# Two attention blocks and a routed expert layer on one core: projections in halves over two steps, a first expert round one step later, group sums copied inside two chains

## The reference, cut to what matters

```python
def reference(x, ...):
    # 1: causal attention over 2048 rows, rotary positions, 16 heads of 8
    x = layernorm(x + attn(x))                 # Q, K, V, softmax(QK/sqrt(8)) V, @ Wo
    # 2: attention over all rows (no mask), then one of 8 experts for each row
    f = x + msa(layernorm(x, ln1), w_qkv, w_proj)
    h = layernorm(f, ln2)
    e = argmax(h @ gate_w + gate_b)            # 8 experts
    f = f + gelu(h @ w1[e]) @ w2[e]            # 128 -> 512 -> 128
    return layernorm(x + f)
```

## Time and profile before

| | |
|---|---|
| median of three runs | 914.34 us (913.54 to 917.52) |
| the profiled execution | 915.0 us, its span 913.3 us (1.7 us lie around it) |
| PE, ACT, DVE, POOL busy | 819.6, 777.6, 328.7, 223.1 us |
| mean granted clock of TensorE | 0.953 of 2.4 GHz |

### The profile page before, as it was taken

One profiled execution on the slowest core, in us unless ns is written; L12 is line 12 of the kernel. 1 busy time (PEld: TensorE's weight loads), 2 busy tenths in 40 slices (PEclk: granted clock), 3 DMA queues, 4 the chain that ended last, 5 costly groups with the idle time before them and its releaser, 6 DMA issues.

```text
span 913.3 us, 24231 instructions
## 1 busy us (share of the span) xinstructions
PE 819.6 (90%) x9924; PEld 372.1 (41%) x9936; DVE 328.7 (36%) x948; ACT 777.6 (85%) x913; POOL 223.1 (24%) x359
## 2 busy tenths in 40 slices
PE   6689899999999999999999999999999999996271
PEld 3344344444444444444343444443444434443231
DVE  3711644410431005330042333264332463334753
ACT  1568789899999999999999999998999999994460
POOL 4732131111100110000003333323234132343333
PEclk9789999999999999999999999999999999998586
DMA  8976120202020250720201000201000010001101
GB/s 264 271 222 197 48 78 17 94 2 48 1 94 1 70 118 2 249 76 2 47 2 32 1 2 4 76 10 33 2 3 19 14 42 2 2 3 31 38 5 41
DMA packets 34357, 51.60 MB, mean 57 GB/s; under 512 B 4032, under 2 KB 14656, under 8 KB 34240
## 3 DMA queue, kind: packets, MB, share of 16 engines
q1 hardware_dynamic: 32704, 46.30, 17.7%
q0 software_dynamic: 1536, 3.67, 1.3%
HBM read 29.12 MB, written 20.84 MB: 55 GB/s over the span
## 4 chain that ended last, share of the span: by engine, by line
PE 58%; issue 21%; DVE 8%; ACT 5%; DMA 3%; POOL 3%; POOLq 2%; ACTq 0%; SPq 0%; DVEq 0%
PE ps L479 54%; ACT probs L864 3%; PE ps L484 2%; POOLq L999 2%; PE ps L738 1%; DMA early_late<-z_sorted 1%; POOL parts L1006 1%; DMA z_sorted<-z_rows,slot_numbers 1%; DVE ln_newton L1068 1%; POOL z_sorted L977 1%; DVE squares_blockdiag L1353 0%; DVE ln_newton L1067 0%; DMA early_late<-in_sin 0%; DVE ln_newton L1066 0%; DVE squares_blockdiag L1352 0%
## 5 line engine op out<-in xcount | busy, mean ns | idle before, releaser
L864 ACT ACTIVATE probs<-ps 128x1024 f32<-128x1024 f32 (+3 forms) x832 | 732.6, 1014 | 52.7 <-PE ps L479 51.0
L479 PE MATMUL ps<-probs,values 128*9 128x256 f32 (+1 forms) x6528 | 429.3, 376 | 4.3 <-POOL probs L972 1.8
L479 PE MATMUL ps<-query_rows,key_rows 32*128 32x512 f32 (+3 forms) x1664 | 289.8, 486 | 16.2 <-ACT probs L864 12.0
L479 PEld LDWEIGHTS ps<-probs,values 128*9 128x9 f32 x6528 | 143.6, 90 | 184.4 <-issue 95.2
L479 PEld LDWEIGHTS ps<-query_rows,key_rows 32*128 32x128 f32 x1664 | 121.6, 183 | 195.2 <-issue 95.3
L972 POOL TENSOR_SCALAR_AFFINE_SELECT probs<-probs 128x256 f32<-128x256 f32 x128 | 53.1, 421 | 238.9 <-ACT probs L864 236.0
L1013 POOL COPY parts<-early_late 128x512 f32 x63 | 42.7, 716 | 147.5 <-PE ps L479 147.4
L977 POOL DMA_INDIRECT z_sorted<-z_rows,slot_numbers x16 | 15.8, 990 | 213.9 <-DVE slot_numbers L1341 204.4
L1209 DVE COPY q_rotated<-ps 128x512 f32<-128x512 f32 x30 | 20.7, 690 | 129.6 <-PE ps L479 129.6
L1006 POOL COPY parts<-parts 128x512 f32 x72 | 45.4, 671 | 29.6 <-PE ps L479 27.8
L1221 DVE RECIPROCAL recip<-ps 128x16 f32<-128x16 f32 x32 | 8.2, 256 | 82.1 <-PE ps L484 82.1
(11 more groups left out here) (171 smaller groups left out, 573.6 us busy)
## 6 DMA issues: line engine op xcount, KB each, us to landing
k_scratch<-parts SPq DMA_DIRECT2D x16, 512.0 KB, 3.8
q_scratch<-parts SPq DMA_DIRECT2D x16, 512.0 KB, 5.1
query_rows<-q_scratch SPq DMA_DIRECT2D x32, 256.0 KB, 5.3
key_rows<-k_scratch SPq DMA_DIRECT2D x20, 256.0 KB, 4.9
key_rows<-k_scratch SPq DMA_DIRECT2D x16, 192.0 KB, 4.5
parts<-in_w SPq DMA_DIRECT2D x1, 2048.0 KB, 8.3
early_late<-in_w SPq DMA_DIRECT2D x8, 256.0 KB, 7.1
early_late<-z_sorted SPq DMA_DIRECT2D x4, 384.0 KB, 3.2
```

The source lines that it names most:

```text
L479: return nc.tensor.matmul(out, l, r, start=start, stop=stop, skip_group_check=True)
L864: nc.scalar.activation(Pr[:, t % KEPT, 2 * p:2 * p + 2, lo:BLK], score_banks(t, p)[:, :, lo:BLK], ACT.Exp, bias=-SHIFT[r["a"]], scale=SCAL ...
```

## The change

- `post_project`, `m_gate` and the three `project2` functions take a half each time: two of four small matmuls, or 256 of 512 columns. The halves stand in two neighbouring steps. For keys, queries and values the second half has the step of `PREP_AT` and the first the step before; `post_project` is at steps 6 and 7 (it was at 6), `m_gate` at 11 and 12 (it was at 11). `m_turn` stays at 10 and `m_ranks` at 13.
- `UP_AT`, `TURN_AT`, `DOWN_AT` of the first round, the second round's `UP_AT` and `DOWN_AT` of the first, and `SORTED_AT`: one step later. Some places of `PREP_AT` too.
- On DVE the group's copy is written at new places: in attention 1 behind `bound_diag` and ahead of the wait for the bound's matmul; in attention 2 after the first of three Newton turns of the row norm, and again after the keys were rounded. A gelu of the expert rounds is written ahead of what is due in the step before `turn`.

```diff
-UP_AT = (25, 31, 38, 44, 50, 57)
+UP_AT = (26, 32, 38, 44, 50, 57)
-SORTED_AT = (22, 23)
+SORTED_AT = (23, 24)
...
+POST_TURN_AT, POST_AT, GATE_AT = 5, 7, 12
...
-            def project2_keys(b):
+            def project2_keys(b, n):
                 s = A[2]
-                turn_taken()
-                pe.wait_ge(hTs, b + 1)
-                mm(ps7, wqkv[:, D:2 * D], hT[:, :]).then_inc(s["k_proj"], 1)
+                c = slice(n * BLK // 2, (n + 1) * BLK // 2)
+                if n == 0:
+                    turn_taken()
+                    pe.wait_ge(hTs, b + 1)
+                last = mm(ps7[:, c], wqkv[:, D:2 * D], hT[:, c])
+                if n == 1:
+                    last.then_inc(s["k_proj"], 1)
...
-                todo = {5: [lambda: post_turn(n - 1)], 6: [lambda: post_project(n - 1)]}
+                todo = {POST_TURN_AT: [lambda: post_turn(n - 1)]}
+                for m in range(2):
+                    todo[POST_AT - 1 + m] = [lambda m=m: post_project(n - 1, (m,))]
...
-                    todo.update({10: [lambda: m_turn(b)], 11: [lambda: m_gate(b)], 13: [lambda: m_ranks(b)]})
+                    todo.update({10: [lambda: m_turn(b)], 13: [lambda: m_ranks(b)]})
+                    for m in range(2):
+                        todo[GATE_AT - 1 + m] = [lambda m=m: m_gate(b, (m,))]
...
-                rsqrt(y, v, h, t, 3)
+                rsqrt(y, v, h, t, 1)
+                between()
+                newton(y, h, t, 2)
...
                 ts(kdg[:, :], ident[0:H, 0:H], u, 1.03, ALU.mult, ALU.mult).then_inc(diag_set, 1)
+                between()
                 dve.wait_ge(bound_mm, a)
...
-                link(layernorm(xb, xb))
+                link(layernorm(xb, xb, lambda: due(10)))
...
                 link(copy(rounded(k3, b), ka[:, :]))
+                due(at[1] + 1)
...
-                        due(at - 1)
+                        due(at - 2)
                         gelu(b, r)
...
-                    bound(1)
+                    bound(1, lambda: due(BOUND1_AT))
```

More of the change, by code:

```diff
@@ L506, in turn_taken, with project2_queries, project2_values @@
                     pe.wait_ge(normed, turns[0])
[L508 removed]
+            def project2_keys(b, n):
                 s = A[2]
[L510 to L520 removed]
+                c = slice(n * BLK // 2, (n + 1) * BLK // 2)
[5 more added lines that the diff above has]
+                    last.then_inc(s["k_proj"], 1)
+            def project2_queries(b, n):
+                s = A[2]
+                c = slice(n * BLK // 2, (n + 1) * BLK // 2)
+                if n == 0:
+                    turn_taken()
+                    pe.wait_ge(s["k_taken"], b + 1)
+                last = mm(ps7[:, c], wqkv[:, 0:D], hT[:, c])
+                if n == 1:
+                    last.then_inc(s["q_proj"], 1)
+            def project2_values(b, n):
                 s = A[2]
[L522 to L524 removed]
+                if n == 0:
+                    turn_taken()
+                    pe.wait_ge(s["q_taken"], b + 1)
+                for i in (2 * n, 2 * n + 1):
                     last = mm(ps[:, 7, i * D:(i + 1) * D], hT[:, i * P:(i + 1) * P], wqkv[:, 2 * D:3 * D])
[L526 removed]
+                if n == 1:
+                    last.then_inc(s["v_proj"], 1)
             def key_norms(a, b):
@@ L670, in post_turn, with post_project @@
                 turned(ps7, lambda i: att[:, i, :]).then_inc(post_t, 1)
-            def post_project(n):
-                pe.wait_ge(post_e, n + 1)
-                for i in range(TB):
+            def post_project(n, halves=(0, 1)):
+                if 0 in halves:
+                    pe.wait_ge(post_e, n + 1)
+                for i in (i for m in halves for i in (2 * m, 2 * m + 1)):
                     last = mm(ps[:, 7, i * D:(i + 1) * D], attT[:, i * P:(i + 1) * P], (wo if n < NB else wproj)[:, :])
-                last.then_inc(post_p, 1)
+                if 1 in halves:
+                    last.then_inc(post_p, 1)
             def z_turn(b):
@@ L687, in m_turn, with m_gate @@
                 turned(ps7, lambda i: zb[:, i, :]).then_inc(m_zT, 1)
-            def m_gate(b):
-                pe.wait_ge(m_h, b + 1)
-                for i in range(TB):
+            def m_gate(b, halves=(0, 1)):
+                if 0 in halves:
+                    pe.wait_ge(m_h, b + 1)
+                for i in (i for m in halves for i in (2 * m, 2 * m + 1)):
                     last = mm(ps[:, 7, i * E:(i + 1) * E], hT[:, i * P:(i + 1) * P], gw[:, :])
-                last.then_inc(m_g, 1)
+                if 1 in halves:
+                    last.then_inc(m_g, 1)
             def m_ranks(b):
@@ L811, in side_of @@
                 b, at = n - 1, PREP_AT[n - 1]
-                ops = (z_turn, project2_keys, project2_queries, project2_values, lambda b: key_norms(2, b), lambda b: query_norms(2, b))
-                for p, f in zip(at, ops):
-                    todo[p] = [lambda f=f: f(b)]
+                for p, f in zip(at[1:4], (project2_keys, project2_queries, project2_values)):
+                    for m in range(2):
+                        todo[p - 1 + m] = [lambda f=f, m=m: f(b, m)]
+                todo.update({at[0]: [lambda: z_turn(b)], at[4]: [lambda: key_norms(2, b)], at[5]: [lambda: query_norms(2, b)]})
                 for i, p in enumerate(at[6]):
@@ L1064, in rsqrt, with newton @@
                 link(ts(h, v, -0.5, None, ALU.mult))
+                newton(y, h, t, turns)
+            def newton(y, h, t, turns):
                 for _ in range(turns):
@@ L1074, in layernorm, with normalize @@
                 link(ins)
-                return normalize(dst, src)
-            def normalize(dst, src):
+                return normalize(dst, src, between)
+            def normalize(dst, src, between=lambda: None):
                 for i in range(TB):
@@ L1130, in take_query_norms, with bound @@
                     link(tt(qmx[:, 0:1], qmx[:, 0:1], qmx[:, 1:2], ALU.max))
-            def bound(a):
+            def bound(a, between=lambda: None):
                 u, y, h, t = (bw[:, m:m + 1] for m in range(4))
@@ L1429, in attention @@
                         dve.sem_inc(mask_free, 1)
-                    due(10)
                     rows_to_h(n - 1, due)
```

8 lines of the change are left out of this document (4 added, 4 removed), and 4 rows, old and new, of the table PREP_AT.

## The result

The changed kernel takes 918.57 us in the median of five executions (918.28 to 926.73) against 914.34 (910.10 to 917.52) in five before, 4.2 us more. The ratio of all executions is 1.0076, with a 95% interval of 1.0044 to 1.0107, so the loss is clear of the noise.

A forecast was written before the change was run, and what follows sets the result against it. ACT was taken to set the pace, 1.83 us a step. Terms -3.1 - 3.1 + 0.6 - 0.7 - 1.15 + 0.8 + 3.6 = -3.05 took 915.0 to 911.95, 911.3 on the median's scale; 8-in-10 range 906.0 to 917.0.

The forecast's parts named there:

- the later round: Attentions 6 to 8, ahead of the second round's turn: the earlier gelu gives 0.1 us each, -0.3 in the sum.
- waits at `m_turn` and at the ranks: Attentions 6 to 8: PE waits 0.8 us at step 10 and 1.7 before the ranks, the latter taken as +1.8 each.
- low stretches behind the ranks: Attentions 6 to 8: a stretch of 0.50 clock follows the ranks' wait, 1.2 us each, +3.6 (bounds 0 and 5).
- Halves: the step that failed most: Splitting PE work over two otherwise plain steps gains about 0.4 us; output projection 2.4 in attentions 3 to 8, projections 1.55.
- I take no wait: Attentions 4 and 5: the first copy is due after the z rows are turned, or with room; attention 4 sums to -0.7.
- Steps 6 to 13 cancel: Attentions 6 to 8, up to step 13: output projection -0.4, wait at `m_turn` +0.8, gate -0.4 us, together 0.
- the three low stretches after the tanh stay: After the gelu's tanh PE idles 1.02 us, then gets 0.50 clock (values 1.90 instead of 1.05 us); this remains three times.
- Attention 2 (-3.1): Attention 2: norm wait about halved (-0.7), copy wait of 1.16 gone, queries -0.5, later halves and norms -0.7; bounds -1.2 and -4.3.
- the clock holds: Rival, chance 0.22: no low stretch after the ranks in attentions 6 to 8, 3.6 us less, 907.7 us.
- the sorted rows late as before: Rival, chance 0.17: the wait at the sorted rows stays in attentions 6 to 8, 4.3 us not gained, 915.6 us.
- Halves bring nothing: Rival, chance 0.13: double weight loads and PE behind through steps 14 to 22 lose the 3.9 us; 913.5 likely, 915.2 at most.

The follow-up runs named there:

- no halves: Kernel before with DVE's moved copies and the round and sorted rows one step later, nothing newly split in halves: 909.49 us, ratio 0.9936.
- gate whole: Changed kernel with the gate alone whole at step 11, output projection still in halves: 916.22 us (1.0006), the second time 911.56 us (0.9973).
- matmuls in the wait: Changed kernel with three unused 128x192 matmuls put in PE's wait before the ranks: 921.82 us, ratio 1.0058 to the kernel before.
- copy ahead: Changed kernel with attention 3's first group copy written ahead of the second norm's last four instructions: 920.69 us, ratio 1.0050 to the kernel before.

## Why the prediction was wrong

It said 911.3 us, the same, range 906.0 to 917.0. Measured are 918.57, 1.6 above the range. The waits that it named came with nearly their size: 0.72 (0.8) at `m_turn`, 1.70 (1.7) at the ranks, 1.17 (1.4) in attention 3, none at the sorted rows in an attention, and the low clock behind the ranks in all three. What failed is the price of the rest. The halves bring half of what it took, a wait in attention 4 was overlooked, and the later round costs where it was to gain. By steps, in us, for the two profiled executions (span +2.9, where the sum said -3.05):

| term | foreseen | measured |
|---|---|---|
| halves: output projection 2.4, projections 1.55, gate 1.2, attention 2 1.2 | -6.35 | -3.2 |
| waits at `m_turn` and at the ranks | +7.8 | +7.8 |
| sorted rows | -4.3 | -4.5 |
| first round one step later | -0.3 | +1.25 |
| waits in attentions 1 and 2 | -3.7 | -3.9 |
| wait in attention 3 | +1.5 | +1.25 |
| wait in attention 4 | 0 | +1.5 |
| **all but the clock** | **-5.35** | **+0.2** |
| low stretches behind the ranks | +3.6 | +3.5 |
| low stretch in attention 1 | -1.3 | -1.6, and +1.5 for a new one |
| low stretch in attention 3 | 0 | +1.5 |
| low stretches after the tanh, and in attention 2 | 0 | -3.1, -1.1 |
| the opening, to step 3 of attention 1 | 0 | +2.2 |
| **the clock** | **+2.3** | **+2.9** |

The measured column adds up to 3.1; the rest is rounding and 0.1 behind the last exponential. That the opening belongs to the clock is read from its longer low stretch and not shown by a run.

- **Halves: the step that failed most (-6.35, measured -3.2).** A split was to be worth 0.4. That of the output projection gained 0.22 (steps 6 and 7: 4.34 to 4.12) and that of the gate 0.32. A half takes 0.65 and not 0.55, so the 0.05 put on it was too small. Its reason, weights loaded again, doesn't hold for these two, and what the rest of a half's time is isn't shown. In attention 5 the halves gave 0.55 instead of 1.15, in attention 2 they cost 0.2 instead of giving 1.2.
- **Attention 4 (-0.7, measured +0.68): a wait overlooked.** "I take no wait" looked at DVE's copies. The first query half landed in the step of the turn, and step 19 took 1.5 more. The run with the queries off the turn took that away.
- **The later round (-0.3, measured +1.25)** in steps 32 to 38, the same in the run of the later round alone (+1.2).
- **Steps 6 to 13 cancel** (-0.4 + 0.8 - 0.4): +0.64 over three attentions, again the size of a split.
- **The clock: one number where there is a spread.** In the profiled pair its sum was near the foreseen one by luck: "the three low stretches after the tanh stay" was wrong (one stayed), and so was the silence on attention 3, and new ones came at other places. In the medians it wasn't: the changed kernel's median execution has 0.009 less clock than that of the kernel before, 5 to 6.6 us, where 2.3 were foreseen. The range had no room for this. With the terms above set right the forecast would have been some 916.8 (an estimate: 911.3 and the 5.55 of the table), still in the range. The 1.7 us that are left are within what the clock differs by.
- **Attention 2 (-3.1)**: -3.04, in part by chance. The two waits gave 2.1 instead of 1.9, the halves cost 0.2, and 1.1 is a low stretch of before, at 76 us, that isn't there after.

Of the rivals, the clock holds fell (both profiles have low stretches behind the ranks), and so did the sorted rows late as before (no wait left). Halves bring nothing had the right direction, but they bring a little, and the waits that they cause, with the low clock behind them, cost nearly five times that (15.5 us against 3.2 in the steps).

The Trainium skill, "TensorE: Matmul & The Clock Gate", section "Loop structure matters more than you think", was weighed with the claim that a DVE copy between groups doesn't take the clock down. Its loop has the next matmuls follow immediately; here PE waited for DVE, so it didn't bear on these places. Not to follow it was right: behind DVE waits of 1.17 and 1.70 us the clock fell to 0.50.

**Open.** Some 0.3% or more of what the output projection's halves cost in the changed kernel (0.6 to 1.1%, against 0.28% alone) is in no step of the profiles. The clock's medians point to it (0.952 and 0.954 with its halves, 0.957 and 0.958 without), but why this kernel falls low more often, outside the waits named, wasn't tried.

## What to carry to other kernels

Before spreading a piece of work over two steps, follow its last result to who waits for it: here the output projection and the gate finished a step later (1.4 us) and gained 0.2 to 0.3, and three of their readers had no slack. A new wait of TensorE can have a low stretch behind it, 0.7 to 2.0 us more, and whether it has is a matter of the place (next section): price it as a chance, and give the range room for as many stretches as the kernel's executions differ by. Of a change of several parts time each alone: two of these gained 0.7% and 0.4%, two lost 0.7% and 0.3%, and the sum hid them all.

## What the runs showed of the hardware

- Whether a wait of PE has a low stretch in or behind it goes by the place, and not by its length alone. Over the 17 profiles of this case: 4 of 4 in attention 1 (1.76 us, for the copy), 7 of 7 in attention 3 (1.15 to 1.17, for the copy), 10 of 12 at the ranks (1.69 to 1.84), 4 of 11 at step 24 of attention 2 (1.4), but none of 4 at step 14 of attention 2 (1.55), none of 4 at its step 18 (1.16, for the copy as in attention 3), and none of 11 at the sorted rows within the attentions (1.03 to 1.64). Why isn't shown.
- At one place it is a matter of chance: behind the wait of 1.02 to 1.04 us for ACT after the tanh a low stretch came in 20 of 51 cases, in all three attentions before, in one after, in none with DVE's moves alone.
- Low stretches come without such a wait too: within the attentions 22 of 69 have no idle time of PE longer than 0.57 us in the 5 us ahead. With DVE's moves alone, attention 3, the clock is 0.50 from 153.6 us on:

```profile
152.74 0.50 PE L479 MATMUL ps<-query_rows,key_rows 32*128 32x512 f32 x2 [0.36 <-ACT probs L864]
153.17 1.49 PE L479 MATMUL ps<-probs,values 128*9 128x256 f32 x16
154.58 1.12 PE L484 MATMUL ps<-ident,z_rows 128*128 128x128 f32 x4
```

- ACT can stand still though the scores that it reads are written, and the clock can fall behind that too. With no halves, attention 8, PE's scores were written by 702.74, ACT idled from 702.94 to 704.46, then PE waited for it and ran low:

```profile
704.46 3.77 ACT L864 ACTIVATE probs<-ps 128x1024 f32<-128x1024 f32 x4 [1.51 <-PE ps L479]
```

```profile
702.24 0.50 PE L479 MATMUL ps<-query_rows,key_rows 32*128 32x512 f32 x4
...
705.53 0.50 PE L479 MATMUL ps<-query_rows,key_rows 32*128 32x512 f32 x2 [1.38 <-ACT probs L864]
705.96 1.60 PE L479 MATMUL ps<-probs,values 128*9 128x256 f32 x16
```

  What held ACT isn't in the trace. Idle times of ACT of 1.2 to 1.7 us at steps 3 to 5 of attentions 7 and 8 stand seven times in the four profiles of one chip (no halves, gate whole the first time, matmuls in the wait, copy ahead) and in none of the 13 others. The kernel before was 1.7 us slower on that chip, but has no profile there, so a part of the gap between the two measurements of gate whole (1.0006 and 0.9973) may be this; it isn't shown.
